# Attention scores from two twelve-bit parts as float32 words in two row tiles, instead of three bfloat16 parts in two column tiles

## What is computed

```python
xn = _ln(x, g1, b1)
q = _lin(xn, Wq, bq).reshape(b, n, H, HD) / np.sqrt(HD)      # H = 16, HD = 8, n = 1024
k = _lin(xn, Wk, bk).reshape(b, n, H, HD)
score = softmax(einsum('bihd,bjhd->bhij', q, k), axis=-1)
v = _lin(xn, Wv, bv).reshape(b, n, R, HD)                    # R = 8
out = einsum('bhij,bjrd->bihrd', score, v)                   # 64 columns per head
```

## Time and profile before

| | |
|---|---|
| median of three runs | 1242.5 us (1242.06 to 1242.65) |
| the profiled execution: its own time / its span | 1243.4 us / 1241.6 us |
| busy share of the span: TensorE, VectorE, GpSimd, ScalarE | 95%, 77%, 77%, 61% |
| weight loads of TensorE | 43% |
| mean granted TensorE clock | 0.977 of 2.4 GHz |

### The profile page before, as it was taken

One profiled execution on the slowest core, in us unless ns is written; L12 is line 12 of the kernel. 1 busy time (PEld: TensorE's weight loads), 2 busy tenths in 40 slices (PEclk: granted clock), 3 DMA queues, 4 the chain that ended last, 5 costly groups with the idle time before them and its releaser, 6 DMA issues. The chain is left out here.

```text
span 1241.6 us, 27803 instructions
## 1 busy us (share of the span) xinstructions
PE 1184.0 (95%) x7997; PEld 538.2 (43%) x7997; DVE 960.4 (77%) x2145; ACT 757.6 (61%) x1463; POOL 956.4 (77%) x561
## 2 busy tenths in 40 slices
PE   5599999999999999999999999999999999977898
PEld 3134444444444444444444444444444444425675
DVE  6676778788888887878788787788878888697752
ACT  3056666666666666667666666666666666644443
POOL 4257898989898988888888889897978888873321
PEclk9589999999999999999999999999999999988999
DMA  4424545454444344444445354544444434330000
GB/s 115 120 65 92 113 95 117 104 116 96 104 102 104 90 113 104 104 106 99 115 99 113 83 116 98 117 105 105 104 104 103 104 88 103 70 68 1 18 25 26
DMA packets 60372, 115.52 MB, mean 93 GB/s; under 512 B 6656, under 2 KB 25568, under 8 KB 60336
## 3 DMA queue, kind: packets, MB, share of 16 engines
q0 software_dynamic: 18784, 67.70, 28.8%
q1 hardware_dynamic: 40770, 47.04, 11.8%
q10 hardware_dynamic: 782, 0.33, 0.1%
HBM read 22.51 MB, written 8.39 MB: 25 GB/s over the span
## 5 line engine op out<-in xcount | busy, mean ns | idle before, releaser
L1234 DVE TENSOR_REDUCE rowmax<-row_bank 128x1 f32<-128x512 f32 x1024 | 662.6, 685 | 191.0 <-PE row_bank L989 182.4
L1181 ACT ACTIVATE prob<-col_bank 128x512 f32<-128x512 f32 x1024 | 555.0, 594 | 273.3 <-PE col_bank L1008 272.1
L1018 PE MATMUL out_bank<-prob,v_op 128*64 128x512 f32 x2048 | 533.3, 594 | 0.4 <-issue 0.2
L1343 POOL TENSOR_TENSOR addend<-prob 128x1024 f32<-128x1024 f32 x128 | 316.4, 2472 | 48.3 <-ACT prob L1181 48.1
L1343 POOL TENSOR_TENSOR quad<-prob 128x1024 f32<-128x1024 f32 x128 | 329.0, 2570 | 28.0 <-ACT prob L1181 27.7
L989 PE MATMUL row_bank<-k_op,q_op 72*64 72x512 bf16 x2048 | 325.7, 388 | 14.6 <-DMA q_op<-q_parts 9.7
L1008 PE MATMUL col_bank<-q_op,k_op 74*64 74x512 bf16 x2048 | 319.5, 383 | 2.2 <-ACT prob L1181 1.2
L1008 PEld LDWEIGHTS col_bank<-q_op,k_op 74*64 74x64 bf16 x2048 | 117.5, 109 | 242.6 <-ACT prob L1181 148.1
L989 PEld LDWEIGHTS row_bank<-k_op,q_op 72*64 72x64 bf16 x2048 | 120.2, 109 | 150.0 <-DVE rowmax L1234 46.3
L1018 PEld LDWEIGHTS out_bank<-prob,v_op 128*64 128x64 f32 x2048 | 151.5, 136 | 71.9 <-issue 11.2
L1348 POOL DMA_DIRECT2D quad<-addend x128 | 112.4, 878 | 77.5 <-POOL addend L1343 73.0
(11 more groups left out here) (197 smaller groups left out, 822.5 us busy)
## 6 DMA issues: line engine op xcount, KB each, us to landing
quad<-addend POOLq DMA_DIRECT2D x128, 512.0 KB, 5.5
v_op<-v_all SPq DMA_DIRECT2D x64, 256.0 KB, 6.5
k_op<-k_parts SPq DMA_DIRECT2D x64, 144.0 KB
q_op<-q_parts SPq DMA_DIRECT2D x192, 48.0 KB
q_parts<-along_parts SPq DMA_DIRECT2D x11, 192.0 KB, 2.1
k_parts<-along_parts SPq DMA_DIRECT2D x33, 64.0 KB, 2.1
out<-y_out SPq DMA_DIRECT2D x8, 256.0 KB, 2.3
q_op<-max_rows SPq DMA_DIRECT2D x64, 4.0 KB
```

Source lines behind the costliest of these rows:

```text
L1018: last = nc.tensor.matmul(out_bank[ih * VW:(ih + 1) * VW, :], v_op[slot][:, t, :], halves(prob[:, t, :])[:, :, ih, :], start=(t == 0), sto ...
L1181: nc.scalar.activation(prob[:, t, h * HALF:(h + 1) * HALF], col_bank[h][:, :], ACT.Exp).then_inc(exp_done, 1)
L1234: nc.vector.tensor_reduce(rowmax[:, parity, t, h:h + 1], row_bank[h][:, :], AX.X, ALU.max).then_inc(max_done, 1)
L1343: pool.tensor_tensor(dst, prob[:, 2 * k, :], prob[:, 2 * k + 1, :], ALU.add).then_inc(pair_done, 1)
```

## The change

q and k are split into two float32 parts of at most twelve significant bits: `high` masks the low 12 bits off with an integer AND (VectorE), `low` subtracts (VectorE in preparation, GpSimd along). Four products of parts make 32 rows; a row of zeros follows, and for column scores the two rows of the maximum, which makes 33 and 35. The matmuls read these words as float32r (one pass) with 128 stationary columns. Slots 0 and 1 stand in partitions 0 to 63, slots 2 and 3 in partitions 64 to 127, so that column scores of unit u and row scores of unit u + 2 lie in different row tiles of the array; for each half h TensorE now issues one column-score and one row-score matmul in turn. The `part` copies are gone, a unit's operands come with three DMAs instead of four, a pair is stored with three instead of four.

```diff
-PARTS = 3
+PARTS = 2
+LOW_BITS = 12
 PROD_ROWS = PARTS * PARTS * HD
 MAX_PARTS = 2
-ROWS = PROD_ROWS + MAX_PARTS
+ROW_ROWS = PROD_ROWS + 1
+ROWS = ROW_ROWS + MAX_PARTS
+ROW_TILE = P // 2
...
-        self.q_op = [sb(f"q_op{s}", [ROWS, SEQ], BF16) for s in range(SLOTS)]
-        self.k_op = [sb(f"k_op{s}", [P, SEQ], BF16) for s in range(SLOTS)]
+        self.q_op = [sb(f"q_op{s}", [P, SEQ]) for s in range(SLOTS // 2)]
+        self.k_op = [sb(f"k_op{s}", [P, SEQ]) for s in range(SLOTS // 2)]
...
+    def q_rows(self, slot, first, end):
+        at = slot // 2 * ROW_TILE
+        return self.q_op[slot % 2][at + first:at + end, :]
...
-        sp.dma_start(self.k_op[slot][0:PROD_ROWS, :], self.k_parts[ds(u, 1)].rearrange("u c d s -> u (c d) s")
+        sp.dma_start(self.k_rows(slot, 0, PROD_ROWS), self.k_parts[ds(u, 1)].rearrange("u c d s -> u (c d) s")
                      .to_broadcast([PARTS, PARTS * HD, SEQ])).then_inc(self.operands_in[slot], DMA)
         for m in range(PARTS):
-            sp.dma_start(self.q_op[slot][m * PARTS * HD:(m + 1) * PARTS * HD, :],
+            sp.dma_start(self.q_rows(slot, m * PARTS * HD, (m + 1) * PARTS * HD),
                          self.q_parts[m, ds(u, 1)].to_broadcast([PARTS, HD, SEQ])).then_inc(self.operands_in[slot], DMA)
...
-    def rest(self, engine, n, c):
+    def high(self, engine, n):
         a = self.at(n)
-        engine.wait_ge(self.part_ready[c], n + 1)
-        done = self.rest_ready if c == 0 else self.part_ready[2]
-        dst = self.full[a][:, :, :] if c == 0 else self.parts[a][:, 0, :, :]
-        engine.tensor_tensor(dst, self.full[a][:, :, :], self.parts[a][:, 2 - c, :, :], ALU.subtract).then_inc(done, 1)
+        engine.wait_ge(self.full_ready, 2 * n + 2)
+        self.wait_left(engine, self.stored, n, STORES * DMA)
+        flat = lambda x: x.rearrange("p m w -> p (m w)").bitcast(I32)
+        engine.tensor_tensor(flat(self.parts[a][:, 0, :, :]), flat(self.full[a][:, :, :]),
+                             self.high_mask.bitcast(I32).to_broadcast([P, 2 * PAIR_COLS]),
+                             ALU.bitwise_and).then_inc(self.part_ready[0], 1)
+    def low(self, engine, n):
+        a = self.at(n)
+        engine.wait_ge(self.part_ready[0], n + 1)
+        engine.tensor_tensor(self.parts[a][:, 1, :, :], self.full[a][:, :, :], self.parts[a][:, 0, :, :],
+                             ALU.subtract).then_inc(self.part_ready[1], 1)
...
-    def part(self, act, n, c):
-
-        if c == 0:
-            act.wait_ge(self.full_ready, 2 * n + 2)
-            self.wait_left(act, self.stored, n, STORES * DMA)
-        else:
-            act.wait_ge(self.rest_ready, n + 1)
-        self.nc.scalar.activation(self.parts[self.at(n)][:, 2 - c, :, :], self.full[self.at(n)][:, :, :],
-                                  ACT.Copy).then_inc(self.part_ready[c], 1)
...
-                last = pool.memset(res.k_op[s][64:P, :], -1.0)
+                at = s // 2 * ROW_TILE
+                pool.memset(res.q_op[s % 2][at + PROD_ROWS:at + ROW_TILE, :], 0.0)
+                last = pool.memset(res.k_op[s % 2][at + PROD_ROWS:at + ROW_TILE, :], -1.0)
...
-            def row_scores(v, slot, t, known_free):
-
-                for h in range(2):
-                    if not known_free:
-                        pe.wait_ge(max_done, 2 * TB * v + 2 * t + h - 1)
-                    for c in range(2):
-                        last = nc.tensor.matmul(row_bank[h][c * VW:(c + 1) * VW, :],
-                                                q_op[slot][0:PROD_ROWS, t * P + c * VW:t * P + (c + 1) * VW],
-                                                k_op[slot][0:PROD_ROWS, h * HALF:(h + 1) * HALF],
-                                                start=True, stop=True)
-                    last.then_inc(row_scored, 1)
+            def row_scores(v, slot, t, h, known_free):
+                if not known_free:
+                    pe.wait_ge(max_done, 2 * TB * v + 2 * t + h - 1)
+                nc.tensor.matmul(row_bank[h][:, :], res.q_rows(slot, 0, ROW_ROWS)[:, t * P:(t + 1) * P].bitcast(FP32R),
+                                 res.k_rows(slot, 0, ROW_ROWS)[:, h * HALF:(h + 1) * HALF].bitcast(FP32R),
+                                 start=True, stop=True).then_inc(row_scored, 1)
...
-            def col_scores(u, slot, t, known_free):
-
-                for h in range(2):
-                    if not known_free:
-                        pe.wait_ge(exp_done, 2 * TB * u + 2 * t + h - 1)
-                    for c in range(2):
-                        last = nc.tensor.matmul(col_bank[h][c * VW:(c + 1) * VW, :],
-                                                k_op[slot][0:ROWS, t * P + c * VW:t * P + (c + 1) * VW],
-                                                q_op[slot][0:ROWS, h * HALF:(h + 1) * HALF],
-                                                start=True, stop=True)
-                    last.then_inc(col_scored, 1)
+            def col_scores(u, slot, t, h, known_free):
+                if not known_free:
+                    pe.wait_ge(exp_done, 2 * TB * u + 2 * t + h - 1)
+                nc.tensor.matmul(col_bank[h][:, :], res.k_rows(slot, 0, ROWS)[:, t * P:(t + 1) * P].bitcast(FP32R),
+                                 res.q_rows(slot, 0, ROWS)[:, h * HALF:(h + 1) * HALF].bitcast(FP32R),
+                                 start=True, stop=True).then_inc(col_scored, 1)
...
-                        col_scores(u, s, t, not before and t == 0)
-                        if ahead:
-                            if t == 0:
-                                pe.wait_ge(operands_in[sv], LOADS * DMA * (Gv + 1))
-                            row_scores(u + 2, sv, t, False)
+                        if ahead and t == 0:
+                            pe.wait_ge(operands_in[sv], LOADS * DMA * (Gv + 1))
+                        for h in range(2):
+                            col_scores(u, s, t, h, not before and t == 0)
+                            if ahead:
+                                row_scores(u + 2, sv, t, h, False)
...
-                        if along and (s, t) == (2, 6):
-                            project.part(act, G, 0)
-                        if along and (s, t) == (3, 6):
-                            project.part(act, G, 1)
...
+                            elif (s, t) == (2, 7):
+                                project.high(dve, G)
...
-                        if along and s == 3 and k in (0, 2):
-                            project.rest(pool, G, k // 2)
+                        if along and s == 3 and k == 2:
+                            project.low(pool, G)
```

More of the change, by code:

```diff
@@ L23 @@
 BF16 = mybir.dt.bfloat16
+FP32R = mybir.dt.float32r
+I32 = mybir.dt.int32
 ALU = mybir.AluOpType
@@ L716, in _ @@
             for n in range(PAIRS_BEFORE):
[L717 removed]
+                project.store(sp, n, n, True, [0], project.stored if n < PAIRS_BEFORE - 1 else last_stored)
             sp.wait_ge(ones_set, 1)
[L719 removed]
+            sp.wait_ge(project.stored, DMA * 2 * (PAIRS_BEFORE - 1))
             sp.wait_ge(k_stored, DMA * (PAIRS_BEFORE - 1))
@@ L724, in _ @@
             sp.wait_ge(x_in[2], DMA)
-            sp.wait_ge(last_stored, DMA * 3)
+            sp.wait_ge(last_stored, DMA * 2)
             sp.wait_ge(last_k_stored, DMA)
@@ L771, in _ @@
             project.take_turned(act, 0)
-            for n in range(PAIRS_BEFORE + 1):
+            for n in range(PAIRS_BEFORE):
                 if n + 1 < PAIRS_BEFORE:
                     project.take_turned(act, n + 1)
-                if n < PAIRS_BEFORE:
-                    for m in range(2):
-                        project.take_qk(act, n, m)
-                    project.part(act, n, 0)
-                if n > 0:
-                    project.part(act, n - 1, 1)
+                for m in range(2):
+                    project.take_qk(act, n, m)
             act.wait_ge(wf_turned, 1)
@@ L871, in _ @@
             last.then_inc(selb_ready, 1)
-            project.rest(dve, 0, 0)
-            project.rest(dve, 1, 0)
-            project.rest(dve, 0, 1)
+            dve.wait_ge(mask_set, 1)
+            project.high(dve, 0)
+            project.low(dve, 0)
+            project.high(dve, 1)
             dve.wait_ge(ws_summed, 1)
@@ L883, in _ @@
             for n in range(1, PAIRS_BEFORE):
+                project.low(dve, n)
                 if n + 1 < PAIRS_BEFORE:
-                    project.rest(dve, n + 1, 0)
-                project.rest(dve, n, 1)
+                    project.high(dve, n + 1)
                 project.take_values(dve, n - 1, (n - 1) * PAIR)
@@ L911, in attention @@
         max_part = lambda parity, m: max_parts[:, parity, m * TB:(m + 1) * TB]
-        max_rows = [sb(f"max_rows{n}", [MAX_PARTS * TB, P], BF16) for n in range(2)]
+        max_rows = [sb(f"max_rows{n}", [MAX_PARTS * TB, P]) for n in range(2)]
         onehot = sb("onehot", [P, SLOTS, 32])
@@ L1120, in _ @@
             for t in range(TB):
-                row_scores(0, 0, t, t == 0)
```

(5 more changed lines are left out.)

32 lines of the change are left out of this document (19 added, 13 removed).

## The result

The changed kernel takes 1284.2 us (median of 4 runs, 1281.7 to 1287.1) against 1242.3 us for the kernel before in the same comparison. The ratio is 1.034 (95% interval 1.032 to 1.036), so it is slower where I had forecast 1189 us, faster. The profiled execution has a span of 1280.0 us against 1241.6 us, 38.4 us more.

A forecast was written before the change was run, and what follows sets the result against it. TensorE was taken to bound the kernel, GpSimd next. Gains of 5 (group 0), 30 (along), 16 (plain) and 4 us (preparation), less 2 (end), made 53 us: 1189 us, range 1165 to 1212 us; 1160 to 1262 us with rivals.

The forecast's parts named there:

- Float32r at the bfloat16 column rate: TensorE's scores: a float32r matmul over 512 columns passes once in 0.215 us, with 0.43 us as the other end.
- Rival 1: TensorE's scores: float32r at 0.43 us or row tiles one after the other, 1380 us; chance 0.16, both 0.01.
- Row tiles side by side: TensorE's scores: two row tiles run beside each other like column tiles; one after the other, 0.86 us per step.
- A change of tiling at 0.147 us: TensorE between scores and values: each change costs 0.147 us, weight load included; 15 more per unit, 2.2 us.
- Rival 2: TensorE's changes of tiling cost more, deciding from 0.23 us; 1303 us at 0.30 us; chance 0.08 to 1260 us, 0.05 beyond.
- The score phase of 0.43 us: TensorE's step: two column-score and two row-score matmuls take 2 x 0.215 = 0.43 us, 0.44 us less per step.
- TensorE's floor: TensorE per group: net 5.2 us less, to 58.0 us (plain) and 60.4 us (along).
- Meeting losses of 0.5 us: Each kind of group: 0.5 us added because three engines stand within 5 us of each other in fixed orders.
- Rival 3: VectorE waits for GpSimd's product, TensorE for the denominators' DMA: 2 us per group more, 32 us, 1221 us; chance 0.12.
- Group 0: Group 0 and its first unit after, 85.2 us before: five units at 1.3 us less the losses, 5 us gained.
- Preparation: Before the first row score: copies, one k store and one q load go, 4 us gained, bounds 1 to 6 us.
- The end: Last two units, no row scores ahead: changes of tiling add 4.7 us, GpSimd's backlog hides some, 2 us lost.

The follow-up runs named there:

- bfloat16 words: Changed kernel with three early full-array matmuls and denominators at t = 7, scores reading only each word's upper half as bfloat16 (lower 16 bits left out): 1217.8 us.
- the wide scores: Kernel before, each pair of 64-column bfloat16 score matmuls made one of 128 columns on the whole array: 1341.4 us, ratio 1.078.
- the denominators moved: Changed kernel with the denominators of the unit before at t = 7 instead of t = 6, transposes staying: 1246.6 us, ratio 1.003.
- the run with the fourth matmul: Changed kernel with denominators at t = 7, three full-array float32 matmuls before group 0 and one more at t = 5 of the first unit: 1232.7 us.
- the kernel with the three matmuls alone: Changed kernel with three float32 matmuls of the whole array over 512 columns ahead of group 0: 1272.0 us, ratio 1.027.

## Why the prediction was wrong, point by point

**Float32r at the bfloat16 column rate: right.** From the second pair to the values pass 0.34 us, and 0.31 us with bfloat16 words; less the 0.11 us of the change of tiling that follows (by the wide scores) a pair's stream is about 0.22 us, an estimate. Rival 1 is out.

**Row tiles side by side: right.** Their starts differ by 0.01 us or less.

**A change of tiling at 0.147 us: right.** From the values to the next scores 1.01 us pass, 0.86 + 0.15; the wide bfloat16 scores in the kernel before gave 0.125 us each. Rival 2 is out by its own bound of 0.23 us, though the time landed near its 1303 us.

**The score phase of 0.43 us: wrong by a term that I left out.** I had counted the weight load inside the price of a change of tiling and asked only what a load costs after a drain. The second pair's load of 128 float32r columns is not behind a change of tiling and is still exposed, by 0.33 - 0.22 = 0.11 us. Streams 0.43 us, this load and the change of tiling behind, 0.12 us, give 0.66 us. That makes the step 1.67 us, not 1.58 us: 0.09 x 32 = 2.9 us per group.

**TensorE's floor.** My 58.0 us per plain group with the 2.9 us added is 60.9 us; with the denominators moved a plain group lasts 61.5 us and TensorE is busy 61.3 us of it. So the floor was sized right but for the load, and TensorE still sets the pace. GpSimd, whose floor of 57.8 us I named as the next bound, never became it.

**Meeting losses of 0.5 us: wrong in size, right in place.** Rival 3 named TensorE's wait for the denominators' DMA behind GpSimd, at 2 us a group. Measured by what the move gives back: 3.4 us per plain group (65.2 us on average against 61.8) and 1.1 us per along one. What no term or rival held is the DMA's own time: in the unit shown TensorE came 0.3 us earlier, and the DMA landed 2.4 us later. GpSimd, idle for exponents 92.4 + 38.4 us against 48.1 + 27.7 us before, is held up by the late TensorE in turn.

**Group 0: the step that failed worst.** I had taken it from rows at full clock, 5 us gained. It took 16.4 us more, because the stream ran at 1.2 GHz for 45.6 us, and group 1 took 9.8 us more, with the second fall of the clock. I never asked whether the new stream would be granted the clock that the old one was, though the profile's clock row and the window (0.97 for group 0) showed that the rise falls inside it. No term of the sum and no rival held it. With the clock kept up, group 0 lasts 81.6 us (69.84 to 151.46 us in the run with the fourth matmul), near the 80.2 us of the forecast.

**Preparation: right.** The first row score starts at 40.49 us, 4.2 us earlier than before. Two of those are lost again to the row scores that stand alone at the start, which step at 1.57 us instead of 1.43 us. **The end:** 3.3 us lost against 2 us.

**Adding up.** The forecast was 53 us gained and the span shows 38.4 us lost, 91.4 us apart. Groups 0 and 1 make 21.4 + 12.8 = 34 us of it, of which some 30 us are the clock (20.0 us in group 0, by the run with the fourth matmul, and up to 10.3 us in group 1, by the later denominators). Without the 34 us the time would be 1250 us, inside the range, and still slower than before where faster was forecast. Preparation and end make 3 us. The other thirteen groups make 54 us. The wait at the denominators, by what the move gives back, is 13.5 + 10.3 = 24 us. Of the remaining 30 us the shorter step with bfloat16 words gave back 12 us, though it is 2.9 us per group or 38 us of TensorE's work. The last 18 us were there even then: they are meeting losses beyond the 0.5 us per group of the forecast, by the pauses that were read there, and how they would divide with float32r is not shown.

**What stays open.** Why the new stream does not raise the clock while its array is busy all the time. Changes of tiling come with a later rise (82 us against 72.6 us in the wide-score kernel). Behind the early pause the bfloat16 words, in the same row tiles of 33 and 35 rows and with the same changes, got the clock back within 11 us, the float32r words only after 30 us at the first denominators. So the words matter, in one execution of each; rows and row tiles were not tried apart. Nor is it shown what makes a pause cost the clock. 0.35 us did not in six executions; 1.39 us did in the profiled one of eleven, and by the times and the mean clock in seven more; but 1.40 and 2.19 us did not in the kernel with the three matmuls alone. And it is open why the DMA lands later after the change.

## What to carry to other kernels

Price every weight load of a new form by itself, not as part of the drain: a load of 128 float32r columns showed 0.11 us in front of its stream where the bfloat16 one showed 0.03 us, between two streams of the same tiling. But don't count on all of a saved load: with it gone, thirteen periods gave back 12 us of the 38 us. Before counting microseconds at full clock, look where in the stream the old kernel got it and whether the new stream has the same work there; four spare matmuls at the start were worth 14 us. When the bounding engine gets faster, list the transfers that it meets at fixed steps, compare for each the time left with the time to landing in both kernels, and try the meeting one step later: that was worth 37.6 us here, 24 us of it in the steady periods.

## What the runs showed of the hardware

TensorE was busy without a gap for 45 us at 1.2 GHz and not given 2.4 GHz; three full-array float32 matmuls ahead of the same stream raised the clock and the stream kept it. Its two stretches at half clock, and the one behind the early pause, ended at a unit's denominators (111.28, 187.43 and 112.70 us). The clock fell behind pauses of 1.39 us and 1.99 us in the new stream, but not behind one of 2.19 us in another run of it, nor behind 1.01 us in the old one. Two row tiles of 64 start together within 0.01 us, and a pair of them streams 512 columns of float32r in about 0.22 us (an estimate from 0.34 us less 0.11 us). The same accumulating DMA of 512 KB, asked for as long ahead, landed in 9.8 us instead of 7.4 us in the changed kernel. The move of a block of work that was free in one tiling pattern (4.93 us for two steps, either way) cost 0.09 us per unit in the other (5.27 us against 5.18 us).
